# Layer 2 attention of a four-layer kernel: scores in two passes, with the maximum carried into the second one by DMA

## The chip, the cores and the metric

The kernel runs on one core of a Trainium2 chip. A core has five engines with a queue each: TensorE (PE in the profile; its weight loads are PEld), VectorE (DVE), ScalarE (ACT), GpSimd (POOL) and SyncE (SP), which here issues the DMAs. The metric is the device time of one execution in microseconds (us); the median of three runs of the kernel before is 3875.83 us.

## The reference, cut to what matters

Four layers run over 4 sequences of 1024 tokens of width 256. The change lies in the attention of the second one (`_L0_ffn_ref`), which has 8 heads of 64 and a causal mask:

```python
sim = jnp.einsum('bhid,bhjd->bhij', q * SCALE, k)
sim = jnp.where(causal_mask, jnp.finfo(sim.dtype).min, sim)
attn = jax.nn.softmax(sim, axis=-1)
out = jnp.einsum('bhij,bhjk->bhik', attn, values)
```

A softmax subtracts the largest score of each query before the exponential. The kernel computes the scores with the keys on partitions, so a query's maximum has to be subtracted along the free axis; it does that inside the matmul sum.

## The kernel before, in words

For each sequence, layer 2 runs three blocks: `gates_and_values`, `attention` and `output_experts`. No engine starts a block before all have finished the one ahead. The change is in `attention`; it adds 8 matmuls at the end of `gates_and_values`.

`attention` first projects two heads at a time: a group c is four products (K and Q, each for 512 tokens), `project` on PE. Each lands in a PSUM bank; ACT rounds it to a shorter format, fp32r (`hi_parts`), and DVE subtracts to get what the rounding lost (`lo_parts`). From the second group on all four products use one bank, so `project` waits for `qk_parts`, the end of DVE's part for the product before it. `kst` holds a head's keys as rounded part in 64 partitions and lost part in the other 64; `qst` holds the rounded queries in both halves; `qlo` the lost part of the queries in both halves.

A head then goes through three kinds of work on PE, each in 8 pieces k = 0 to 7, one per 128 keys or queries:

- `maxima` (L648, L650): rounded scores of 128 queries against the keys up to them, 1024 columns at k = 0 down to 128 at k = 7. DVE reduces each to one number per query (L769, `mx`).
- `scores` (L662 to L666): 12 units of up to 512 columns for the 8 pieces, 1024 columns at k = 0 down to 128 at k = 7. Each unit is a product with `qst` (L662), a product with `qlo` (L663), on the diagonal the mask (L665), and a product of `negones` with `shift` (L666), which subtracts the maximum. `shift` is a diagonal matrix of the maxima that POOL writes from `mx` (L785), eight instructions per head. ACT takes the exponential (L703, `prob`).
- `weighted` (L674): `prob` times the values in full fp32, into bank `PV`. At a head's end ACT copies the row of denominators (`den_out`, L725) and DVE the output (`head_out`, L759); the next head's first `weighted` waits for both.

The order is written out by hand on every engine. Step by step, the scores of one head run in the same step as the maxima of the next, piece by piece, and in every second step the four projections of a later group lie between them. A head's scores follow its last maxima directly, in the next step. Where the text says "step of head h" it means from the first score product of h to that of h+1: projections fall in those of heads 0, 2 and 4, and no maxima are left in that of head 7.

PE waits in its own queue for `shift_ready` before a head's first score, for `exp_ready` (three banks) before later ones, and for `max_read` before a piece of maxima, since those share two pairs of half-banks.

Layer 3 has a step of the same sort as the one that the change brings here. Its SP queue moves maxima out of a column of `peak` into one row of `qst` (L1274), 128 elements of 4 bytes per DMA and 8 DMAs in a row; its products L1303 then wait for them.

Of the kernel before, what the change touches and what calls it, by code (L numbers as in the profile page):

```python
# [421 lines left out]
ATTN2 = ("qk_mm qk_hi qk_parts max_mm max_read shift_ready score_mm exp_ready pv_mm o_read den_read "  # L422
# [6 lines left out]
def layer2(nc, ctx, m, I, src, dst):  # L429
# [39 lines left out]

    def gates_and_values(own):  # L470
# [14 lines left out]
        with nc.Block() as block:  # L485
# [7 lines left out]
            def _(pe):  # L493
# [7 lines left out]
                for n, (h, t) in enumerate(order):  # L501
# [10 lines left out]
                    last.then_inc(s.value_mm, 1)  # L512

# [76 lines left out]
    def attention(own, b):  # L590
# [6 lines left out]
        mx = sb("mx", [P, H0, NT])  # L597
# [5 lines left out]
        parts = [(kind, n) for kind in "kq" for n in range(NH)]  # L603
        part_at = {0: 0, 1: 1, 2: 2, 4: 3}
# [10 lines left out]
        with nc.Block() as block:  # L615
            @block.sync
            def _(sp):
                fetch_load(sp, m, s, src[(b + 1) % SEQS])
                sp.dma_start(oe[:, :, :], I["oe2"][:, 0]).then_inc(s.oe_in, 16)
                for h in range(H0):  # L620
                    sp.wait_ge(s.den_read, h + 1)
                    sp.dma_start(dens[h:h + 1, :], den[den_row(h), h % 2, :]).then_inc((s.even_den_out, s.odd_den_out)[h % 2], 16)
                sp.wait_ge(s.even_den_out, 16 * (H0 // 2))
                sp.wait_ge(s.odd_den_out, 16 * (H0 // 2))
                sp.wait_ge(s.oe_in, 16)

            @block.tensor
            def _(pe):
# [10 lines left out]
                def maxima(h, k):  # L639
                    t = NT - 1 - k  # L640
                    if k == 0:
                        pe.wait_ge(s.qk_parts, 4 * (h // 2 + 1))
# [10 lines left out]
                def scores(h, k):  # L653
                    for n, (kk, lo, hi) in enumerate(units, U * h):
                        if kk != k:
                            continue
                        if n % U == 0:
                            pe.wait_ge(s.shift_ready, NT * (h + 1))
                        if n >= 3:
                            pe.wait_ge(s.exp_ready, n - 2)  # L660
                        out, keys = bank(m.ps, n % 3, 0, hi - lo), kst[:, h % RK, k * P:(k + 1) * P]
                        pe.matmul(out, keys, qst[:, h % RK, lo:hi], start=True, stop=False)  # L662
# [15 lines left out]
                for step in range(H0 + 2):  # L678
                    h1, h2 = step - 1, step - 2
                    for k in range(NT):  # L680
                        if h2 >= 0:
                            scores(h2, k)
                        if step % 2 == 0 and step < H0 and k in part_at:
                            project(step // 2, part_at[k])
                        if 0 <= h1 < H0 and k < NT - 1:
                            maxima(h1, k)
                        if h2 >= 0 and k >= 1:
                            weighted(h2, k - 1)
                        if 0 <= h1 < H0 and k == NT - 2:
                            maxima(h1, NT - 1)  # L690
                    if h2 >= 0:
                        weighted(h2, NT - 1)

            @block.scalar
            def _(act):
# [10 lines left out]
                def hi_parts(c, j):  # L706
# [5 lines left out]
                    for odd in (0, 1):  # L712
                        got, slot = bank(m.ps, proj_bank(c, j), 0, HALF, half(odd)), (2 * c + odd) % RK
                        if kind == "k":
                            last = act.copy(kst[half(odd), slot, cols], got)
# [11 lines left out]
                for step in range(H0 + 2):  # L727
                    h2 = step - 2
                    for k in range(NT):
                        if h2 >= 0:  # L730
                            exps(h2, k)
                        if k == 0 and h2 >= 1:
                            den_out(h2 - 1)
                        if k == 3 and step == H0 + 1:
                            fetch_sd(act, m, s)
                        if step % 2 == 0 and step < H0 and k in part_at:
                            hi_parts(step // 2, part_at[k])
# [3 lines left out]
            def _(dve):  # L741
                def lo_parts(c, j):
# [3 lines left out]
                    for odd in (0, 1):  # L746
# [4 lines left out]
                        else:  # L751
                            for to in (0, 1):
                                last = dve.tensor_tensor(qlo[half(to), slot, cols], got, qst[half(odd), slot, cols].bitcast(F32),
                                                         ALU.subtract)
# [6 lines left out]
                for step in range(H0 + 2):  # L761
                    h1, h2 = step - 1, step - 2
                    for k in range(NT):
                        if k == 0 and h2 >= 1:
                            head_out(h2 - 1)
                        if 0 <= h1 < H0:
                            t = NT - 1 - k
                            dve.wait_ge(s.max_mm, NT * h1 + k + 1)
                            dve.reduce_max(mx[:, h1, t:t + 1], bank(m.ps, max_bank(h1, k), 0, (t + 1) * P), AX_X).then_inc(s.max_read, 1)  # L769
                        if step % 2 == 0 and step < H0 and k in part_at:  # L770
                            lo_parts(step // 2, part_at[k])
# [5 lines left out]
            def _(pool):  # L777
                clear(pool, s1)
                for h in range(H0):
                    if h >= 2:  # L780
                        pool.wait_ge(s.score_mm, U * (h - 1))
                    for k in range(NT):
# [1111 lines left out]
```

## Time and profile before

| | |
|---|---|
| median of 3 runs | 3875.83 us (3875.41 to 3878.35) |
| profiled execution: time | 3882.36 us |
| profiled execution: span | 3880.6 us |
| PE busy | 3373.7 us, 87% |
| DVE / ACT / POOL busy | 2080.9 / 1466.3 / 830.2 us |
| layer 2's attention, four times | 206.1, 206.8, 205.2 and 206.5 us |
| of these, PE busy | 188.5, 189.2, 187.6 and 188.9 us |

The profile gives the share of the span in which each engine worked, groups of instructions by line, and, for any stretch, the instructions in order of time with the idle time before each and what ended it. The granted clock (PEclk) is the share of TensorE's full speed that the chip gave in a stretch: 1.00 is 2.4 GHz and 0.50 is 1.2 GHz. Matmul ends are modelled: a 512-column product is shown with 0.39 us, while the next one starts 0.23 us after it, so the cost of a product on PE is the distance between two starts. Below that is called its slot.

### The profile page before, as it was taken

Reading aid. Unit: us, or ns where it says so; the run is one execution under the profiler, and the core shown is the slowest. Engines: PE = TensorE matmul, PEld = TensorE weight load, DVE = VectorE, ACT = ScalarE, POOL = GpSimd, SP = SyncE. Lnnn points to the kernel's source line nnn. Section 1 sums busy time; section 2 is a strip of 40 time slices with the busy share of each in tenths; the row PEclk is TensorE's granted clock in tenths of the full one; section 3 lists DMA queues with packets and bytes.
Section 4 is the critical chain, followed back from the end, with each engine's and each line's share of the span. In section 5 each row is a group of like instructions: output and inputs, shape, how many; then the busy total and the mean of one; then the engine's idle time right before and its main releaser. Section 6 shows DMA issues by size and latency. Waiting matters only on the chain. (4 is left out here: it accounts for less than half of the span.)

```text
span 3880.6 us, 51281 instructions
## 1 busy us (share of the span) xinstructions
PE 3373.7 (87%) x18610; PEld 2435.7 (63%) x18610; DVE 2080.9 (54%) x3463; ACT 1466.3 (38%) x2638; POOL 830.2 (21%) x908
## 2 busy tenths in 40 slices
PE   6996898988988989888989698998988789888898
PEld 4555655975568755875569445555454477777776
DVE  4446744686455954667446574655647434343333
ACT  2321144412443134421444355463644433333333
POOL 1112322742246411643127101001010000000000
PEclk9997899988998999998999789898998899899999
DMA  5111100110011100210001200000001120000000
GB/s 179 41 45 60 38 1 30 45 45 22 1 51 47 44 1 1 74 34 33 1 30 48 63 2 13 12 7 18 2 12 12 61 94 6 17 11 12 11 12 11
DMA packets 139735, 121.01 MB, mean 31 GB/s; under 512 B 79696, under 2 KB 121936, under 8 KB 136016
## 3 DMA queue, kind: packets, MB, share of 16 engines
q1 hardware_dynamic: 139472, 117.45, 9.9%
q8 instruction: 172, 2.82, 0.3%
q14 instruction: 91, 0.75, 0.1%
HBM read 100.23 MB, written 28.31 MB: 33 GB/s over the span
## 5 line engine op out<-in xcount | busy, mean ns | idle before, releaser
L1375 ACT ACTIVATE l3b_prob<-sums 128x512 f32<-128x512 f32 (+3 forms) x768 | 337.8, 497 | 280.7 <-PE sums L1308 224.3
L1623 PE MATMUL sums<-l4a_uhi,l_h 128*128 128x512 f32 x1024 | 405.2, 396 | 0.0
L1623 PE MATMUL sums<-l4a_ulo,l_h 128*128 128x512 f32 x1024 | 404.0, 395 | 0.0
L842 POOL TENSOR_TENSOR l2c_rlo<-l2c_routed,l2c_rhi 128x512 fp32r<-128x512 f32 x256 | 348.1, 1373 | 216.0 <-ACT l2c_rhi L868 178.6
L769 DVE TENSOR_REDUCE l2b_mx<-sums 128x1 f32<-128x1024 f32 (+7 forms) x256 | 192.1, 758 | 316.5 <-PE sums L650 315.8
L703 ACT ACTIVATE l2b_prob<-sums 128x512 f32<-128x512 f32 (+3 forms) x384 | 186.4, 491 | 394.8 <-PE sums L666 390.0
L1668 DVE TENSOR_TENSOR l4a_ulo<-l4a_made,l4a_uhi 128x512 fp32r<-128x512 f32 x192 | 132.3, 689 | 375.2 <-ACT l4a_uhi L1636 374.3
L222 POOL COPY sb_x<-sb_nx 128x2048 f32<-128x2048 f32 x12 | 23.0, 1914 | 1383.6 <-issue 604.6
L952 PE MATMUL sums<-l2c_ohi,l2c_rhi 128*128 128x256 f32 x1024 | 295.2, 288 | 12.8 <-POOL l2c_rlo L842 11.9
L1303 PE MATMUL sums<-l_qst,l_kst 64*128 64x512 f32 (+3 forms) x768 | 290.6, 440 | 17.2 <-DMA l_qst<-l3b_peak 9.9
L674 PE MATMUL sums<-l2b_prob,l_vx 128*128 128x512 f32 (+3 forms) x768 | 301.0, 506 | 3.3 <-ACT l2b_den L725 1.9
L952 PE MATMUL sums<-l2c_ohi,l2c_rlo 128*128 128x256 f32 x1024 | 292.7, 286 | 0.0
L952 PE MATMUL sums<-l2c_olo,l2c_rhi 128*128 128x256 f32 x1024 | 292.6, 286 | 0.0
L1286 PE MATMUL sums<-l_kst,l_qst 64*128 64x512 f32 (+3 forms) x768 | 244.5, 459 | 46.7 <-DVE l3b_peak L1387 21.6
L785 POOL TENSOR_SCALAR l2b_shift<-sb_ident,l2b_mx 128x128 fp32r<-128x128 f32 x256 | 154.2, 605 | 603.7 <-DVE l2b_mx L769 494.3
L905 DVE TENSOR_TENSOR l2c_routed<-l_oT,sums 128x512 f32<-128x512 f32 x256 | 171.7, 683 | 151.3 <-PE sums L942 148.0
L1303 PEld LDWEIGHTS sums<-l_qst,l_kst 64*128 64x128 f32 x768 | 147.2, 207 | 162.0 <-ACT l3b_prob L1375 130.7
L868 ACT CAST l2c_rhi<-l2c_routed 128x512 fp32r<-128x512 f32 x256 | 158.1, 621 | 239.9 <-DVE l2c_routed L905 238.9
L203 PE MATMUL sums<-sb_ident,sb_nx 128*128 128x128 f32 x256 | 61.1, 422 | 193.2 <-issue 92.7
L1623 PEld LDWEIGHTS sums<-l4a_uhi,l_h 128*128 128x128 f32 x1024 | 192.3, 188 | 47.3
L1623 PEld LDWEIGHTS sums<-l4a_ulo,l_h 128*128 128x128 f32 x1024 | 192.3, 188 | 46.1
L510 PE MATMUL sums<-l2a_vhi,l2a_xhi 128*128 128x512 f32 x512 | 204.8, 400 | 10.7 <-POOL l2a_vlo L574 6.3
(247 smaller groups left out, 8170.7 us busy)
## 6 DMA issues: line engine op xcount, KB each, us to landing
l_ve<-ve SPq DMA_DIRECT2D x34, 512.0 KB, 4.1
l_oe<-oe SPq DMA_DIRECT2D x16, 1024.0 KB, 5.9
sb_nx<-sums SPq DMA_DIRECT2D x15, 1024.0 KB, 5.6
l2c_word<-weights_copy SPq DMA_DIRECT2D x32, 352.0 KB, 3.6
weights_copy<-h SPq DMA_DIRECT2D x2, 4096.0 KB, 26.2
l_qst<-l3b_peak SPq DMA_DIRECT2D x512, 0.5 KB, 2.0
l_h<-weights_copy SPq DMA_DIRECT2D x2, 4096.0 KB, 23.9
sb_nx<-tokens SPq DMA_DIRECT2D x5, 1024.0 KB, 5.6
```

The costliest lines, as they stand in the source:

```text
L510: last = pe.matmul(bank(m.ps, n % RING), x[:, c, t * P:(t + 1) * P], v[:, h % 2, c, :], start=(c == 0 and x is xhi and v is vhi), stop=(c ...
L674: last = pe.matmul(bank(m.ps, PV, lo, hi), vx[:, k, h, :], prob[:, k % 2, lo:hi], start=(k == 0), stop=True, skip_group_check=True)
L703: act.activation(prob[:, k % 2, lo:hi], bank(m.ps, n % 3, 0, hi - lo), ACT.Exp, scale=SCALE0).then_inc(s.exp_ready, 1)
L769: dve.reduce_max(mx[:, h1, t:t + 1], bank(m.ps, max_bank(h1, k), 0, (t + 1) * P), AX_X).then_inc(s.max_read, 1)
L842: pool.tensor_tensor(rlo[:, i % RT, :], routed[:, i % RT, :], rhi[:, i % RT, :].bitcast(F32), ALU.subtract).then_inc(s.routed_lo, 1)
L868: act.copy(rhi[:, i % RT, :], routed[:, i % RT, :]).then_inc(s.routed_hi, 1)
L905: dve.tensor_tensor(routed[:, i % RT, :], oT[:, c, n * HALF:(n + 1) * HALF], bank(m.ps, 4 + i % 4), ALU.mult).then_inc(s.routed, 1)
L952: last = pe.matmul(m.ps[:, t * D:(t + 1) * D], r[:, k % RT, cols], w[:, c % 2, e, :], start=(c == e == 0 and t % 2 == 0 and r is rhi and w ...
L1286: last = pe.matmul(bank(m.ps, at, 0, hi - lo), qst[rows(a), p, t * P:(t + 1) * P], kst[rows(a), p, lo:hi], start=True, stop=True)
L1303: last = pe.matmul(bank(m.ps, part % SCORE, 0, hi - lo), kst[rows(a), p, k * P:(k + 1) * P], qst[rows(a), p, lo:hi], start=True, stop=True)
L1375: act.activation(prob[:, i % RB, j, a, 0:hi - lo], bank(m.ps, part % SCORE, 0, hi - lo), ACT.Exp, scale=SCALE1).then_inc(s.exp_ready, 1)
L1623: run(lambda out, a, x, first, last: pe.matmul(out, a, x, start=first, stop=last))
```

## The change

The product with `qlo` and the product of `negones` with `shift` become one. `krow` holds the rounded keys of a head in partitions 0 to 63 and the constant -1 in partition 64; `qrow` holds the lost part of the queries in 0 to 63 and the maxima, as a row, in 64. One product over these 65 partitions (L701) adds the lost part and subtracts the maximum. (Lost part times lost part, which the `qlo` product had as well, is no longer in the sum.)

- PE: 12 products fewer per head. Maxima of a head end two pieces ("ticks", `WAIT = 2`) before its scores start.
- SP: 8 new DMAs per head (L651) take a column of `mx`, 128 elements of 4 bytes in 128 partitions, to a stretch of the row. The first waits until all eight maxima of the head are read; the head's first score waits for all eight to land. The DMA of the denominators stands behind them.
- POOL: its 8 instructions per head and the tile `shift` go; one memset per sequence writes the row of -1.
- ACT: four copies instead of two per K product (`kst` and `krow`). DVE: two subtractions instead of four per Q product. The products go in the order K0, K1, Q1, Q0, in ticks 2 to 5 instead of 0, 1, 2 and 4.
- DVE's `head_out` and ACT's `den_out` stand behind the reduction and the copies of their tick; before, they stood ahead of them (`den_out` ahead of the copies).
- The first head's maxima wait for all rounded parts and two lost parts, no longer for all four lost parts.
- PE gets 8 products that nobody reads (`warm`) at the end of `gates_and_values`, 8 behind the first four projections, and one behind each piece of the first head's maxima.

```diff
-        kst, qst, qlo = (sb(n, [P, RK, T], F32R) for n in ("kst", "qst", "qlo"))
-        shift = sb("shift", [P, 2, T], F32R)
+        kst, qst = sb("kst", [P, RK, T], F32R), sb("qst", [P, RK, T], F32R)
+        krow, qrow = sb("krow", [P, RK, T], F32R), sb("qrow", [P, RK, T], F32R)
+        ROWS = DH0 + 1
...
-        parts = [(kind, n) for kind in "kq" for n in range(NH)]
-        part_at = {0: 0, 1: 1, 2: 2, 4: 3}
+        parts = [("k", 0), ("k", 1), ("q", 1), ("q", 0)]
+        WAIT = 2
+        part_at = {WAIT + j: j for j in range(4)}
+        ticks = NT * (H0 + 2) + WAIT + 1
+        scored_in = lambda x: divmod(x - 2 * NT - WAIT, NT)
+        peaked_in = lambda x: divmod(x - NT, NT)
...
+                for h in range(H0):
+                    sp.wait_ge(s.max_read, NT * (h + 1))
+                    if h >= 2:
+                        sp.wait_ge(carried[h % 2], carried_to(h - 2))
+                    if h >= RK:
+                        sp.wait_ge(s.score_mm, U * (h - RK + 1))
+                    for t in range(NT):
+                        sp.dma_start(qrow[DH0:ROWS, h % RK, t * P:(t + 1) * P].bitcast(F32),
+                                     mx[:, h, t:t + 1].bitcast(F32)).then_inc(carried[h % 2], 16)
+                    if h >= 1:
+                        den_row_out(h - 1)
...
                         if n % U == 0:
-                            pe.wait_ge(s.shift_ready, NT * (h + 1))
+                            pe.wait_ge(s.qk_parts, 4 * (h // 2 + 1))
+                            pe.wait_ge(carried[h % 2], carried_to(h))
+                            pe.wait_ge(s.row_ready, 1)
...
-                        pe.matmul(out, keys, qlo[:, h % RK, lo:hi], start=False, stop=False)
...
-                        pe.matmul(out, m.negones[:, :], shift[:, h % 2, lo:hi], start=False, stop=True).then_inc(s.score_mm, 1)
+                        pe.matmul(out, krow[0:ROWS, h % RK, at], qrow[0:ROWS, h % RK, lo:hi], start=False,
+                                  stop=True).then_inc(s.score_mm, 1)
...
+                for x in range(ticks):
+                    h2, k2 = scored_in(x)
+                    h1, k1 = peaked_in(x)
+                    if has(h2):
+                        scores(h2, k2)
+                    if project_in(x):
+                        project(*project_in(x))
+                        if x == 3:
+                            warm(pe, 6, 8)
+                    if has(h1):
+                        maxima(h1, k1)
+                        if h1 == 0:
+                            warm(pe, PROJ, 1)
+                    h2, k2 = scored_in(x - 1)
+                    if has(h2):
+                        weighted(h2, k2)
...
+                            act.copy(kst[half(odd), slot, cols], got)
+                            last = act.copy(krow[half(0), slot, cols], got)
...
+                            last = dve.tensor_tensor(qrow[half(0), slot, cols], got, qst[half(odd), slot, cols].bitcast(F32),
+                                                     ALU.subtract)
...
+                    if has(h1):
+                        t = NT - 1 - k1
+                        dve.wait_ge(s.max_mm, NT * h1 + k1 + 1)
+                        dve.reduce_max(mx[:, h1, t:t + 1], bank(m.ps, max_bank(h1, k1), 0, (t + 1) * P), AX_X).then_inc(s.max_read, 1)
+                    if project_in(x):
+                        lo_parts(*project_in(x))
+                    if k2 == 0 and 1 <= h2 < H0:
+                        head_out(h2 - 1)
```

What PE's queue holds where one head's scores end and the next head's begin. Before: the last maxima of the next head (L648 with 128 columns), the last score unit of this one, two weighted products (L674), and the next head's first scores.

```order
L648 MATMUL sums<-l2b_kst,l2b_qst 128x128
L650 MATMUL sums<-sb_mask_qk,sb_ident 128x128
L662 MATMUL sums<-l2b_qst,l2b_kst 128x128
L663 MATMUL sums<-l2b_qlo,l2b_kst 128x128
L665 MATMUL sums<-sb_mask_kq,sb_ident 128x128
L666 MATMUL sums<-l2b_shift,sb_negones 128x128
L674 MATMUL sums<-l2b_prob,l_vx 128x256
L674 MATMUL sums<-l2b_prob,l_vx 128x128
L662 MATMUL sums<-l2b_qst,l2b_kst 128x512
```

After, at the same place; the next head's last maxima (L682 with 128 columns) stand seven rows higher still, with a weighted product of 512 columns and the score unit of 256 columns behind them.

```order
L684 MATMUL sums<-sb_mask_qk,sb_ident 128x128
L710 MATMUL sums<-l2b_prob,l_vx 128x384
L698 MATMUL sums<-l2b_qst,l2b_kst 128x128
L700 MATMUL sums<-sb_mask_kq,sb_ident 128x128
L701 MATMUL sums<-l2b_qrow,l2b_krow 128x128
L682 MATMUL sums<-l2b_kst,l2b_qst 128x512
L682 MATMUL sums<-l2b_kst,l2b_qst 128x384
L684 MATMUL sums<-sb_mask_qk,sb_ident 128x128
L710 MATMUL sums<-l2b_prob,l_vx 128x256
L698 MATMUL sums<-l2b_qst,l2b_kst 128x512
```

Between a head's last maxima and its first scores there now lie two ticks: three weighted products, two score units and the first two pieces of the maxima of the head after it.

SP's queue in the attention block. Before, after the two large loads there are only the rows of the denominators:

```order
L121 ISA
L121 DMA sb_nx<-sums 128x8x256
L619 DMA l_oe<-oe 128x2048
L622 DMA l_dens<-l2b_den 1x16x64 [waits l2_attn_den_read] x8
L615 UNCONDITIONAL_BRANCH [waits l2_attn_oe_in,l2_attn_odd_den_out,l2_attn_even_den_out]
```

After, heads 0 and 1, and the start of head 2:

```order
L639 DMA l_oe<-oe 128x2048
L651 DMA l2b_qrow<-l2b_mx 1x128x1 [waits l2_attn_max_read]
L651 DMA l2b_qrow<-l2b_mx 1x128x1 x7
L651 DMA l2b_qrow<-l2b_mx 1x128x1 [waits l2_attn_max_read]
L651 DMA l2b_qrow<-l2b_mx 1x128x1 x7
L642 DMA l_dens<-l2b_den 1x16x64 [waits l2_attn_den_read]
L651 DMA l2b_qrow<-l2b_mx 1x128x1 [waits l2_attn_even_carried,l2_attn_max_read]
```

Eight issues with one wait ahead of them came in per head, and each row of denominators now stands behind the next head's eight.

## Rows read from the trace of the kernel before

**Rows 1.** Stretches: start:end and length, busy us (count) by engine, PEclk, DMA

```profile
448.80:472.90 24.10, 15.73 (x36) 7.79 (x36) 14.11 (x20) 6.96 (x12) 4.79 (x8) 0.71 0.26 87
...
571.40:600.40 29.00, 26.23 (x107) 15.06 (x105) 15.63 (x22) 13.74 (x25) 4.79 (x8) 1.00 0.00 1
600.40:619.10 18.70, 18.70 (x88) 11.92 (x88) 7.11 (x9) 6.79 (x13) 4.85 (x8) 1.00 0.00 1
...
637.90:654.90 17.00, 16.16 (x70) 10.11 (x68) 8.18 (x30) 9.54 (x16) 0.00 (x0) 1.00 0.01 1
```

**Rows 2.** Timeline of PE: start us, us, instruction, idle before; first scores of head 5

```profile
600.38 0.50 PE L662 MATMUL sums<-l2b_qst,l2b_kst 128*128 128x512 f32 x1 [0.19 <-POOL l2b_shift L785]
600.72 0.39 PE L663 MATMUL sums<-l2b_qlo,l2b_kst 128*128 128x512 f32 x1
600.96 0.23 PE L665 MATMUL sums<-sb_mask_kq,sb_ident 128*128 128x128 bf16 x1
```

**Rows 3.** Timeline of PE: the end of the same step

```profile
611.93 0.80 PE L662 MATMUL sums<-l2b_qst,l2b_kst 128*128 128x512 f32 x1
...
615.49 1.08 PE L674 MATMUL sums<-l2b_prob,l_vx 128*128 128x512 f32 x2
616.00 0.68 PE L662 MATMUL sums<-l2b_qst,l2b_kst 128*128 128x256 f32 x1
616.52 0.28 PE L663 MATMUL sums<-l2b_qlo,l2b_kst 128*128 128x256 f32 x1
616.64 0.23 PE L665 MATMUL sums<-sb_mask_kq,sb_ident 128*128 128x128 bf16 x1
...
619.14 0.50 PE L662 MATMUL sums<-l2b_qst,l2b_kst 128*128 128x512 f32 x1
```

**Rows 4.** Layer 3's carry on SP: timeline, and the landing times of line L1274

```profile
2229.97 4.98 SPq L1274 DMA_DIRECT2D l_qst<-l3b_peak  x8
...
2236.40 0.47 SPq L1274 DMA_DIRECT2D l_qst<-l3b_peak  x1
...
DMA to landing us min/median/max: 1.9/2.0/3.9
```

**Rows 5.** Instructions of head 5's step by shape: busy us, mean ns, idle before

```profile
L759 DVE COPY l_oT<-sums 64x1024 f32<-64x1024 f32 x1 | 1.2, 1217 | 1.0 <-PE sums L674 1.0
...
L769 DVE TENSOR_REDUCE l2b_mx<-sums 128x1 f32<-128x768 f32 x1 | 1.0, 958 | 2.3 <-PE sums L650 2.3
```

**Rows 6.** Timeline of all engines: projections and last maxima, head 4's step

```profile
578.18 1.98 PE L635 MATMUL sums<-l_xT,l_wk 128*128 128x512 f32 x4 [1.34 <-DVE l2b_kst L749]
...
590.78 1.88 PE L635 MATMUL sums<-l_xT,l_wq 128*128 128x512 f32 x4
...
592.69 2.36 ACT L718 CAST l2b_qst<-sums 64x512 fp32r<-64x512 f32 x4 [1.12 <-PE sums L635]
...
595.08 2.79 DVE L753 TENSOR_TENSOR l2b_qlo<-sums,l2b_qst 64x512 fp32r<-64x512 f32 x4 [1.39 <-ACT l2b_qst L718]
...
598.69 0.23 PE L650 MATMUL sums<-sb_mask_qk,sb_ident 128*128 128x128 bf16 x1
...
598.96 0.29 DVE L769 TENSOR_REDUCE l2b_mx<-sums 128x1 f32<-128x128 f32 x1 [0.16 <-PE sums L650]
```

**Rows 7.** Stretches, columns as in rows 1: around two idle stretches of PE

```profile
2361.00:2363.30 2.30, 0.67 (x10) 0.58 (x11) 0.00 (x0) 0.89 (x3) 0.00 (x0) 1.00 0.07 1
2363.50:2366.70 3.20, 3.20 (x28) 2.10 (x24) 0.00 (x0) 2.29 (x6) 0.00 (x0) 0.50 0.00 0
3410.00:3412.50 2.50, 0.00 (x0) 0.00 (x0) 2.50 (x8) 0.00 (x0) 0.00 (x0) 1.00 0.06 21
3412.70:3416.00 3.30, 3.30 (x15) 2.67 (x16) 3.30 (x6) 3.20 (x6) 0.00 (x0) 1.00 0.00 0
```

**Rows 8.** Timeline: the first head's maxima and their reductions, sequence 1

```profile
463.84 1.22 PE L648 MATMUL sums<-l2b_kst,l2b_qst 128*128 128x512 f32 x2 [6.38 <-DVE l2b_qlo L753]
...
465.23 2.22 DVE L769 TENSOR_REDUCE l2b_mx<-sums 128x1 f32<-128x1024 f32 x2 [1.45 <-PE sums L650]
```

More of the change, by code:

```diff
@@ L468, in layer2, with warm @@
     fetch_first(nc, m, s0, src[0], load, prepare)
+    def warm(pe, at, times):
+        for _ in range(times):
+            pe.matmul(bank(m.ps, at), sel[:, 0, :], sel[:, 0:HALF // P, :], start=True, stop=True)
     def gates_and_values(own):
@@ L602, in attention, with project_in @@
         through = lambda k: sum(kk <= k for kk, _lo, _hi in units)
-        parts = [(kind, n) for kind in "kq" for n in range(NH)]
-        part_at = {0: 0, 1: 1, 2: 2, 4: 3}
+        parts = [("k", 0), ("k", 1), ("q", 1), ("q", 0)]
[4 more added lines that the diff above has]
+        peaked_in = lambda x: divmod(x - NT, NT)
+        has = lambda h: 0 <= h < H0
+        carried = (s.even_carried, s.odd_carried)
+        carried_to = lambda h: 16 * NT * (h // 2 + 1)
+        def project_in(x):
+            step, k = divmod(x, NT)
+            if x < 4:
+                return 0, x
+            if step and step % 2 == 0 and step < H0 and k in part_at:
+                return step // 2, part_at[k]
         MAX, PV, PROJ = 3, 5, 7
@@ L725, in den_out @@
                     act.copy(den[den_row(h), h % 2, :], bank(m.ps, PV, 0, T, den_row(h))).then_inc(s.den_read, 1)
[L727 to L737, printed above, removed]
+                for x in range(ticks):
+                    h2, k2 = scored_in(x)
+                    if has(h2):
+                        exps(h2, k2)
+                    if project_in(x):
+                        hi_parts(*project_in(x))
+                    if k2 == 0 and 1 <= h2 < H0:
+                        den_out(h2 - 1)
+                    if (h2, k2) == (H0 - 1, 3):
+                        fetch_sd(act, m, s)
                 den_out(H0 - 1)
@@ L759, in head_out @@
                     dve.tensor_copy(oT[vcol(h), h // 2, :], bank(m.ps, PV, 0, T, vcol(h))).then_inc(s.o_read, 1)
[L761 to L771, printed above, removed]
+                for x in range(ticks):
+                    h2, k2 = scored_in(x)
+                    h1, k1 = peaked_in(x)
+                    if has(h1):
+                        t = NT - 1 - k1
+                        dve.wait_ge(s.max_mm, NT * h1 + k1 + 1)
+                        dve.reduce_max(mx[:, h1, t:t + 1], bank(m.ps, max_bank(h1, k1), 0, (t + 1) * P), AX_X).then_inc(s.max_read, 1)
+                    if project_in(x):
+                        lo_parts(*project_in(x))
+                    if k2 == 0 and 1 <= h2 < H0:
+                        head_out(h2 - 1)
                 fetch_stats(dve, m, s)
@@ L778, in _ @@
                 clear(pool, s1)
[L779 to L782, printed above, removed]
-                        t = NT - 1 - k
-                        pool.wait_ge(s.max_read, NT * h + k + 1)
-                        pool.tensor_scalar(shift[:, h % 2, t * P:(t + 1) * P], m.ident[:, :], mx[:, h, t:t + 1], None,
-                                           ALU.mult).then_inc(s.shift_ready, 1)
+                pool.memset(krow[DH0:ROWS, :, :].bitcast(F32), -1.0).then_inc(s.row_ready, 1)
     def output_experts(own, b):
```

34 lines of the change are left out of this document (9 added, 25 removed).

## The prediction

> **What bounds the kernel now.** I read the stretches of layer 2's attention first [rows 1]. The step of head 5, without projections, lasts 18.7 us and PE is busy in all of it; ACT works 6.8 us of it, DVE 7.1. So PE sets the pace there, and a product less is time won as long as nothing makes PE wait. The step of head 4, with four projections, lasts 29.0 us and leaves PE idle for 2.8; the timeline names the rounding of the projections for half of that [rows 6]. The head of the block takes 24.1 us at a mean granted clock of 0.71. The last step, 17.0 us, has scores and weighted products alone. Per sequence that is the head, one step of 32 us (head 0), two of 29, four of 18.75, and 17: 206 us. Then I read what the new wait will cost, from the place in layer 3 where the same transfer is made [rows 4], and how the clock answers idle stretches [rows 7].
>
> **The product that goes.** A lost-part product of 512 columns has a slot of 0.24 us (600.72 to 600.96) [rows 2], one of 256 has 0.12 [rows 3]; those of 384 and 128 are taken as 0.18 and 0.11. A head has 6, 2, 2 and 2 of them: 1.44 + 0.24 + 0.36 + 0.22 = 2.25 us. That lies on PE, the bound, and 32 heads make 72 us. The product with the row of maxima takes the place of the one with `shift`: as many columns, so no change. POOL's eight instructions go, and with them the wait of about 0.2 us at a head's first score [rows 2]. A step without projections thus holds 18.75 - 2.25 - 0.2 = 16.3 us of PE work. The memset of the -1 row, 4096 elements in one partition, would take 5 us at the rate of DVE's copy of 1024 [rows 5] and runs on an idle POOL during the 24 us of the head.
>
> **The carry that comes.** From the last maxima product of a head to its reduced maximum pass 0.56 us (598.69 to 598.96, and 0.29 more) [rows 6]. SP then issues eight DMAs. Layer 3 does exactly this: eight issues take 4.98 us, one every 0.64, each lands 2.0 us after its issue, and the next group, which waits for the last landing, starts 6.43 us after the first [rows 4]. Shape and size are the same (128 elements of 4 bytes from 128 partitions into one row), so I take 6.43. With 0.1 at each end for the hand-over, as between PE and DVE in rows 6, the next head's first score starts 7.1 us after the last maxima product ends. Cover: before, 3.65 us lie between 615.49 and 619.14 [rows 3]. The two ticks that now stand there hold the same weighted products and score units without two lost-part products (0.23), without the smaller maxima of 256 and 128 columns (0.35) and the last weighted product (0.3), but with the maxima of 1024 and 896 columns, four products of 0.23 or less and two masks, 1.0 together: 3.8 us. Exposed at each head: 7.1 - 3.8 = 3.3 us. That is more than the 2.25 won. Behind PE's wait stand the next maxima, so DVE and ACT stand too, and nothing catches up later.
>
> **The weighted product's wait.** `head_out` now stands behind the reduction of 768 columns in its tick. From the first score: scores 1.05 and maxima 0.43, 0.2 to hand over, 0.96 and 1.22 on DVE [rows 5], so the head's first weighted product can start 3.9 us in; PE would be there at 3.2. It costs 0.7 in steps without projections; where projections hold PE up anyway, nothing.
>
> **Steps without projections** (heads 1, 3, 5, 6): 16.3 + 3.3 + 0.7 = 20.3 against 18.75: +1.55, four of them +6.2.
>
> **Steps with projections.** All four share a bank, so the next starts only when the rounding of the last is through. In rows 6 the fourth starts at 590.78, DVE's part at 595.08, 4.30 later, behind four ACT copies. The change makes that four copies for every product and two DVE subtractions (half of the 2.79): 4.30 + 1.40 + 0.05 = 5.75 us from start to start. PE's own work between two projections is 3.7 to 5.2 us, so the chain bounds. Before, a K product needed two copies only. The step: 1.05 of scores, three times 5.75, the fourth projection 1.75, then what PE still has to do up to the last maxima, about the 4.1 us of 611.93 to 616.00 [rows 3], which holds the same kinds of work; then 7.1 for the carry: 31.2 against 29.0, +2.2. For heads 2 and 4 that is +4.4.
>
> **The last step** has no carry behind it: 17.0 - 2.1 = 14.9 (0.1 of the 2.25 kept for its waits on exponentials).
>
> **The head.** The maxima wait for ACT's last copy and no longer for DVE's last subtraction, and DVE's queue is two subtractions shorter per Q product. The reductions begin at about 463.2 instead of 465.23 [rows 8], and the clock may be up for the first projections thanks to the unread products, 1.6 us more in perhaps half the cases. The reductions then end near 469.5 and the carry brings the first score to 475.6, against 472.9 [rows 1]: +2.7. The unread products themselves stand in waits of 4 to 6 us. Head 0's step is 31.2 and some 2 us for a low clock after the idle carry, against 30.6 to 32.0: +1.9.
>
> Sum per sequence: 2.7 + 1.9 + 6.2 + 4.4 - 2.1 = 13.1; four make +52 us.
>
> **The clock.** PE now idles some 3 us before every head's first score. In the trace such stretches have gone both ways [rows 7]: after an idle stretch of 1.9 us ending at 2362.6 the clock was 0.50 for the next 3.2 us, with PE busy throughout; after 2.85 us ending at 3412.6 it stayed at 1.00. Of 17 idle stretches of 1.9 to 2.9 us, 10 were followed by a fall; of nine of 3.0 to 3.4 all were. A fall costs half of some 3.4 us, 1.7, less the 0.7 of the weighted product's wait, which it hides. I take 1 us for each of seven heads: +7 per sequence, +28. Bounds: nothing, and 2.5 us per head where two stretches in a row are slow, +70.
>
> In all +80 us. The profiled execution would go from 3882.4 to 3962; the median of the runs, 6.5 us lower, from 3875.8 to **3956**.
>
> **A rule against the measured rows.** By the trace a group of eight is in place after 6.4 us [rows 4]. The Trainium skill, "DMA: Bandwidth & Descriptors", section "Rules for kernel authors", says to issue a DMA early and wait late, since its fixed setup cost overlaps with compute. Read as one fixed cost for the group, the carry would fit under two ticks and the sum would be that of the first rival; the rows show the issues in series instead.
>
> **Rivals.** (1) The carry is hidden: the issues are short here and the group lands 2.1 us after its start. The gap is then 2.8 us, less than the cover of 3.8; steps without projections fall to 17.0 (-7.0 for four), those of heads 2 and 4 to 28.2 (-1.6), the last to 14.9 (-2.1), the head gains 1.6 and head 0's step 1.1: -13.4, four times -54: **3822**. It decides from an issue of (3.8 - 2.8) / 7 = 0.14 us down. For it speaks only that SP has little else to do; against it, 512 issues of 0.6 us. Chance 0.08. (2) The carry is exposed but the clock holds, as at 3412: 3876 + 52 = **3928**. Chance 0.22. (3) Every stall brings two slow stretches, and the waits of 1 to 2 us in the projections bring more: +52 + 90 = **4018**. Chance 0.12. (4) Carry half hidden, gains and losses level: within 8 us of 3876. Chance 0.04. The forecast itself: 0.54.
>
> **Numbers.** Median 3956. The forecast and rival 2 lie between 3910 and 3985 with their unknowns (0.7 or nothing for the weighted product, 6.4 or the 7 us of a disturbed group, 0.5 to 1.5 us of clock per head); a part of rival 3 is taken in: 3908 to 4005. Faster by over 0.2% (8 us, what a measurement can tell): 0.08; within: 0.04; slower: 0.88.
>
> **What would show it.** Right: SP with eight issues of 0.6 us behind each head's last maximum; PE idle for about 3 us before L698 of each head, ended by the DMA to `l2b_qrow`; steps of 20 to 22 and 31 to 34 us; a PEclk under 1.00 in the attention's middle; PE busy some 60 us less in all, clock apart. Wrong: issues of 0.1 us, or a first score that waits for nothing; then it is rival 1. If the steps with projections are much shorter than 31 us, my chain through the rounding is mis-sized.

## The result, and the profile after

The changed kernel takes 3966.5 us (median of four runs, 3961.4 to 3970.5) where the kernel before takes 3875.6 (3869.5 to 3878.4): a ratio of 1.0236, with 1.0218 to 1.0254 as the interval. It is slower, and the forecast of 3956 was 10 us short. The profiled execution has a span of 3968.7 us against 3880.6.

First the page's totals of after: busy time, share of the span, instructions.

```profile
span 3968.7 us, 50755 instructions
...
PE 3363.5 (85%) x18322; PEld 2402.9 (61%) x18322; DVE 2034.3 (51%) x3399; ACT 1498.2 (38%) x2702; POOL 688.9 (17%) x656
```

PE runs 288 instructions fewer than before (18322 against 18610) and is busy 10 us less (3373.7 before), yet the span is 88 us longer. So PE works less and waits more. Attention, from the first projection to the last weighted product, went from 206.1, 206.8, 205.2 and 206.5 us in the four sequences to 227.8, 228.7, 232.1 and 229.1: +93 us in all. The rest of the kernel is 5 us shorter; in it layer 3, whose code did not change, is 10 us shorter and the other parts together 5 longer.

The stretches of sequence 1 in the columns of [rows 1], which they answer: the head of the block, then the steps of heads 0, 3, 4, 5 and the last one; behind them 3.2 us shortly after head 3's first score, the end of head 4's step, and the 3.3 us behind that.

```profile
451.50:477.70 26.20, 18.39 (x58) 9.39 (x58) 13.51 (x18) 9.08 (x16) 3.50 (x1) 0.91 0.26 80
477.80:513.10 35.30, 28.07 (x90) 14.26 (x91) 11.47 (x16) 14.84 (x28) 0.00 (x0) 0.88 0.02 1
567.20:588.20 21.00, 18.18 (x76) 11.04 (x77) 7.18 (x9) 6.78 (x13) 0.00 (x0) 0.92 0.03 1
588.20:621.20 33.00, 26.02 (x92) 13.45 (x93) 12.69 (x17) 15.72 (x29) 0.00 (x0) 0.95 0.02 1
621.30:641.50 20.20, 16.88 (x76) 9.84 (x76) 7.09 (x9) 6.67 (x13) 0.00 (x0) 1.00 0.03 0
662.00:679.30 17.30, 16.53 (x58) 9.89 (x58) 8.17 (x30) 9.64 (x16) 0.00 (x0) 0.84 0.01 1
568.60:571.80 3.20, 3.20 (x13) 2.44 (x12) 2.08 (x2) 2.41 (x5) 0.00 (x0) 0.50 0.00 0
618.80:621.10 2.30, 0.00 (x0) 0.00 (x0) 0.57 (x1) 0.00 (x0) 0.00 (x0) 1.00 0.10 1
621.30:624.60 3.30, 3.30 (x18) 2.29 (x18) 1.62 (x2) 2.40 (x4) 0.00 (x0) 1.00 0.00 0
```

In [rows 1] the step of head 5 had PE busy for all of its 18.7 us. Now it is busy for 16.9 of 20.2: less work, more time. The last three rows are the clock's: PE does nothing for 2.3 us before head 5's first score and goes on at full clock; before head 3's it idles as long (2.49 us, next view), and the clock is 0.50 in the 3.2 us shown, with PE busy throughout.

The timeline around head 3's first score (all engines, shortened) shows what PE waits for. It answers [rows 3] for the cover and [rows 4] for the carry.

```profile
560.07 0.23 PE L684 MATMUL sums<-sb_mask_qk,sb_ident 128*128 128x128 bf16 x1
560.14 1.08 PE L710 MATMUL sums<-l2b_prob,l_vx 128*128 128x512 f32 x2
560.65 0.68 PE L698 MATMUL sums<-l2b_qst,l2b_kst 128*128 128x256 f32 x1
560.67 4.98 SPq L651 DMA_DIRECT2D l2b_qrow<-l2b_mx  x8
561.41 0.64 PE L682 MATMUL sums<-l2b_kst,l2b_qst 128*128 128x512 f32 x2
562.16 1.22 DVE L803 TENSOR_REDUCE l2b_mx<-sums 128x1 fp32r<-128x1024 f32 x1 [1.52 <-PE sums L684]
563.44 0.68 PE L682 MATMUL sums<-l2b_kst,l2b_qst 128*128 128x512 f32 x2 [0.37 <-DVE l2b_mx L803]
564.02 0.65 PE L710 MATMUL sums<-l2b_prob,l_vx 128*128 128x256 f32 x2
567.16 0.47 PE L698 MATMUL sums<-l2b_qst,l2b_kst 128*128 128x512 f32 x1 [2.49 <-issue]
```

The last maxima product of head 3 starts at 560.07. SP begins its eight issues at 560.67 and spends 4.98 us on them. The last transfer lands at 567.07, 6.40 after the first issue, and PE's first score follows at 567.16. PE's own work for the two ticks between ran out at 564.67. The page labels the 2.49 us "<-issue", that is, it names no releaser; the landing is known from the records of the DMA, and where PE stands at the same wait in experiment 4, the page names the DMA to `l2b_qrow`. From L684 to L698 pass 7.09 us here, and 7.05 to 7.15 at 30 of the 32 heads.

Before head 7's first score PE idles longer, 4.17 to 4.19 us in all four sequences, though the carry takes no longer:

```profile
657.17 0.65 PE L710 MATMUL sums<-l2b_prob,l_vx 128*128 128x256 f32 x2
662.00 0.77 PE L698 MATMUL sums<-l2b_qst,l2b_kst 128*128 128x512 f32 x1 [4.18 <-issue]
```

No head follows, so no maxima lie in the two ticks and the cover is shorter. For the same reason head 6's step holds less work than those of heads 1, 3 and 5.

All issues together, by count and with the least, the median and the longest duration in ns, and the time from issue to landing:

```profile
L651 SPq DMA_DIRECT2D l2b_qrow<-l2b_mx x256: 469/601/1373, 471.2 to 2081.7; - x128
...
DMA to landing us min/median/max: 1.9/2.0/2.8
```

The other two waits that the prediction names. The first is in head 6's step; the kernel lets this weighted product start only behind `head_out` (L795), `den_out` and the exponentials of its piece:

```profile
644.29 1.23 DVE L795 COPY l_oT<-sums 64x1024 f32<-64x1024 f32 x1
...
645.62 0.67 PE L710 MATMUL sums<-l2b_prob,l_vx 128*128 128x512 f32 x1 [0.68 <-ACT l2b_prob L740]
```

The page names ACT, but the copy L795 ends at 645.52 and PE starts 0.10 later; `den_out` ended at 644.57 and the exponentials of the piece at 643.49. So it is `head_out` that PE waits for. The second is in head 4's step:

```profile
592.93 0.58 ACT L752 CAST l2b_kst<-sums 64x512 fp32r<-64x512 f32 x1 [2.46 <-PE sums L668]
...
594.60 0.58 ACT L753 CAST l2b_krow<-sums 64x512 fp32r<-64x512 f32 x1
...
595.21 1.39 DVE L786 TENSOR_TENSOR l2b_kst<-sums,l2b_kst 64x512 fp32r<-64x512 f32 x2 [0.90 <-ACT l2b_krow L753]
...
596.66 0.70 PE L668 MATMUL sums<-l_xT,l_wk 128*128 128x512 f32 x1 [2.12 <-DVE l2b_kst L786]
```

DVE can begin only at 595.21, behind the copies into `kst` and into `krow`, and the next projection waits 2.12 us for it at 596.66. In [rows 6] the like wait was 1.34.

### The profile page after: what moved, and what is told of

It is laid out like the page before. It is cut to its first block and busy times, and to the rows that moved or that the text cites. A ratio compares the mean times of both kernels' runs of the same rounds, so it can differ in the third digit from the quotient of the medians.

```text
span 3968.7 us, 50755 instructions
## 1 busy us (share of the span) xinstructions
PE 3363.5 (85%) x18322; PEld 2402.9 (61%) x18322; DVE 2034.3 (51%) x3399; ACT 1498.2 (38%) x2702; POOL 688.9 (17%) x656
## 5 line engine op out<-in xcount | busy, mean ns | idle before, releaser
L803 DVE TENSOR_REDUCE l2b_mx<-sums 128x1 fp32r<-128x1024 f32 (+7 forms) x256 | 191.8, 756 | 425.8 <-PE sums L684 424.9
L710 PE MATMUL sums<-l2b_prob,l_vx 128*128 128x512 f32 (+3 forms) x768 | 311.0, 516 | 4.8 <-ACT l2b_prob L740 4.8
L698 PE MATMUL sums<-l2b_qst,l2b_kst 128*128 128x512 f32 (+3 forms) x384 | 225.8, 588 | 91.8 <-issue 91.8
```

The lines of the kernel that those rows point to most:

```text
L698: pe.matmul(out, kst[:, h % RK, at], qst[:, h % RK, lo:hi], start=True, stop=False)
L710: last = pe.matmul(bank(m.ps, PV, lo, hi), vx[:, k, h, :], prob[:, k % 2, lo:hi], start=(k == 0), stop=True, skip_group_check=True)
```

## The experiments

**1. Is it the carry's place, or its being there at all?** Each DMA is issued as soon as its own maximum is read, from the largest piece down. The DMA of a head's denominators, which stood behind the eight, moves with them: it now stands in the middle of a later head's.

```
             for h in range(H0):
-                sp.wait_ge(s.max_read, NT * (h + 1))
...
-                for t in range(NT):
+                for k in range(NT):
+                    t = NT - 1 - k
+                    sp.wait_ge(s.max_read, NT * h + k + 1)
                     sp.dma_start(qrow[DH0:ROWS, h % RK, t * P:(t + 1) * P].bitcast(F32),
...
-                    if h >= 1:
-                        den_row_out(h - 1)
+                        if k == 3 and h >= 2:
+                            den_row_out(h - 2)
+                den_row_out(H0 - 2)
...
```

> The changed kernel with one edit: each of a head's eight DMAs is issued as soon as its own maximum is read, instead of all eight behind the last one. Theory A (the eight issues in series behind the last maximum are what costs, 7.1 us from the last maxima product to the first score against 3.8 us of cover): only the last issue and its landing remain behind the last maximum, 0.56 + 0.6 issued and landed in 2.0, so about 2.8 us, less than the cover. PE no longer idles before a head's first score; 3.3 us and the low clock go at seven heads, somewhat more at the first, four sequences: 3825 to 3860 us. Theory B (the stall is only where other costs of the new order show, such as the longer rounding chain or the later output copies): PE waits elsewhere instead and the time stays above 3900 us.

Measured: 3839.8 us against 3872.5, a ratio of 0.992 (0.990 to 0.994). The moment at which the same 256 DMAs are issued turns 91 us of loss into 33 of gain. The timeline at the same place of a step (sequence 2, before head 2):

```profile
959.74 0.66 PE L684 MATMUL sums<-l2b_kst,l2b_qst 128*128 128x512 f32 x2 [0.37 <-DVE l2b_mx L805]
959.76 0.47 SPq L652 DMA_DIRECT2D l2b_qrow<-l2b_mx  x1
...
960.31 0.65 PE L712 MATMUL sums<-l2b_prob,l_vx 128*128 128x256 f32 x2
...
960.61 0.58 PE L700 MATMUL sums<-l2b_qst,l2b_kst 128*128 128x512 f32 x1
```

No idle time stands before the first score of any head. The steps of heads 1, 3 and 5 take 17.6 us, that of head 6 16.1, those of heads 2 and 4 28.6 to 30.3. From the last maxima product to the first score now pass 4.25 us (2.6 for head 7) instead of 7.09. The rows of the denominators were moved too, and that part wasn't tried apart; but in after PE starts 0.1 us behind the landing of the eighth DMA, and no score waits for a row of denominators. Attention is 194 to 198 us per sequence instead of 228 to 232.

**2. Is it an amount of cover?** The issue stays late, and the distance from a head's last maximum to its scores grows from two ticks to three.

```
-        WAIT = 2
-        part_at = {WAIT + j: j for j in range(4)}
+        WAIT = 3
+        part_at = {2 + j: j for j in range(4)}
```

> The changed kernel with three ticks instead of two between a head's last maxima and its first scores; the projections stay in ticks 2 to 5 and the eight DMAs stay behind the last maximum. Theory A: the chain stays 7.1 us, the cover grows from 3.8 to 5.7 us, so about 1.4 us stay exposed in steps without projections and none where a projection falls into the third tick; with fewer falls of the clock some 70 us less than the changed kernel, 3880 to 3915 us. Theory B: no change beyond 10 us, since the wait moves to another place.

Measured: 3885.9, a ratio of 1.0031 (1.0012 to 1.005). A tick more takes back 81 us. Steps without projections are 18.2 to 18.9 us; idle stretches of 0.9 to 2.2 are left before some first scores and one of 2.6 before head 7's. Both runs say that the exposed carry, with what hangs on it, is the loss.

**3. Does the price go by issues or by bytes?** Every DMA is cut in two of 64 elements: the same bytes, 16 issues a head.

```
                 for t in range(NT):
-                    sp.dma_start(qrow[DH0:ROWS, h % RK, t * P:(t + 1) * P].bitcast(F32),
...
+                    for part in (0, 1):
+                        at = t * P + HPART * part
+                        sp.dma_start(qrow[DH0:ROWS, h % RK, at:at + HPART].bitcast(F32),
...
```

> The changed kernel with each DMA of the carry split into two of 64 elements, sixteen per head. If an issue costs 0.64 us whatever it moves, the chain grows by 8 x 0.64 = 5.1 us per head, 32 heads 164 us: 4120 to 4150 us. If an issue costs by the element, the sixteen take as long as the eight: 3960 to 3975 us.

Measured, one run: 4151.3 us, 185 above after, for 256 issues more. A half costs as much to issue as a whole:

```profile
L653 SPq DMA_DIRECT2D l2b_qrow<-l2b_mx x512: 463/597/1630, 472.2 to 2263.2; - x171
```

597 ns against 601. From the last maxima product to the first score pass 11.9 us instead of 7.1: eight issues more take 4.8, 0.60 each, or 154 us for 32 heads. So the price is one of issues. The other 31 fit the clock, which is at 0.50 for 85 to 102 us of attention per sequence instead of 34 to 51.

**4. What does the clock take?** Ten unread products stand ahead of each head's wait for the carry, so that PE is busy where it would idle. The time of the carry isn't touched.

```
                             pe.wait_ge(s.qk_parts, 4 * (h // 2 + 1))
+                            warm(pe, PROJ, 10)
                             pe.wait_ge(carried[h % 2], carried_to(h))
```

> The changed kernel with ten more unread products on PE ahead of each head's wait for the carried row (2.3 us at full clock, inside the wait of 2.5 us and more). The wait itself stays. Clock theory: nothing falls any more before heads 1 to 6, steps without projections go from 21.05 to 20.32 us, and the falls in the steps with projections and at the first head are fewer: 25 to 40 us less than the changed kernel, 3926 to 3942 us. Rival: the clock costs nothing, since other waits absorb it: 3960 to 3970 us.

Measured: 3940.3, a ratio of 1.0174 (1.0155 to 1.0192): 26 us under after. The steps of heads 0, 1 and 2 in sequence 2, columns as in [rows 1]:

```profile
941.05:972.36 31.31, 26.44 (x100) 14.39 (x100) 11.47 (x16) 14.71 (x28) 0.00 (x0) 1.00 0.02 0
972.36:992.72 20.36, 19.28 (x87) 11.83 (x87) 7.09 (x9) 6.67 (x13) 0.00 (x0) 1.00 0.03 1
992.72:1024.06 31.34, 26.67 (x103) 14.62 (x103) 12.70 (x17) 15.61 (x29) 0.00 (x0) 1.00 0.02 1
```

With the clock at 1.00 a step without projections is 20.36 us and one with them 31.3, whereas after has 21 to 22 and 33 or more where the clock fell. Of the 91 us the falls that went are thus worth 26 by the medians; attention alone is 36 us shorter in the profiled executions (881 against 918 in all). Neither is the whole price of the clock: 7 of 30 falls behind the first head's first score are left, and the unread products push that first score back by 0.9 to 1.1 us (8.02 to 8.23 from the last maxima product instead of 7.12 to 7.15). The rest, 57 to 65 us, is waits, less the product's gain.

**5. What is the removed product worth?** The kernel before, without its product with `qlo`. It leaves the lost part of the queries out of the scores, and nothing comes in its place.

```
                        pe.matmul(out, keys, qst[:, h % RK, lo:hi], start=True, stop=False)
-                       pe.matmul(out, keys, qlo[:, h % RK, lo:hi], start=False, stop=False)
```

> The kernel before without the product of keys with the lost part of the queries, which is left out of the sum; all else is as before. It prices the product alone. Theory A (PE is the bound and each head's twelve products are worth 2.25 us): 32 x 2.25 = 72 us less, 3800 to 3812 us. Theory B (maxima, exponentials or the projections' rounding take over as the bound): less than half of that, above 3840 us.

Measured: 3841.7, a ratio of 0.9917 (0.9895 to 0.9938): 31 us, not 72. A step without projections falls by 1.63 us (18.75 to 17.12), not by 2.25; one with projections by 0.64 (28.98 to 28.34), since there other waits grow, those for the roundings and for the reductions: PE's idle time in such a step goes from 2.8 to 3.8 us. In head 3's step the clock fell in each sequence (18.4 to 18.5 us at a mean of 0.91), which takes most of the gain back there. PE's waits over about 120 us of sequence 2 (us in total, times, longest), in this kernel:

```profile
PE sums L648 <- DVE l2b_mx L768: 4.0, 5, 1.5
```

and in the kernel before:

```profile
PE sums L648 <- DVE l2b_mx L769: 2.5, 2, 1.3
```

With less to do between, PE comes to the next maxima before DVE has read the last. One such place, timeline of PE and DVE in sequence 1:

```profile
599.31 1.22 DVE L768 TENSOR_REDUCE l2b_mx<-sums 128x1 f32<-128x1024 f32 x1 [0.95 <-PE sums L650]
...
600.59 0.67 PE L648 MATMUL sums<-l2b_kst,l2b_qst 128*128 128x512 f32 x2 [0.31 <-DVE l2b_mx L768]
```

The next maxima start when the 1.22 us reduction ends, and PE has stood 0.31. In the kernel before, the lost-part products filled that: such a step had no idle time at all. From start to start this one place takes 0.40 us more than before, which is two thirds of the 0.6 by which 1.63 falls short of the slots.

**6. The unread products, under a late carry.** After, without them.

```
-                warm(pe, 7, 8)
...
-                        if x == 3:
-                            warm(pe, 6, 8)
...
-                        if h1 == 0:
-                            warm(pe, PROJ, 1)
```

> The changed kernel without the unread products. Prediction's view: they stand in waits and only lift the clock for the first projections, 1.6 us in half the cases, so without them 0 to 4 us more per sequence: 3966 to 3982 us. Rival: they delay the first head's maxima, since one stands behind each piece, and the time falls to 3950 to 3962 us.

Measured: 3984.0, a ratio of 1.0278 (1.0254 to 1.0302), 17 us over after. The profiled executions agree on the direction only: layer 2 is 4 us longer, and layer 3, whose code is the same in both, 16 (948.6 against 932.9). All four runs are slower than all four of after, but only 4 us are found in the layer that was edited. So neither the size nor, for certain, the sign is shown here; experiment 9 is the better test.

**7. The copy into `krow` moved to GpSimd.** It copies from `kst`, as soon as ACT has rounded, and leaves ACT two copies per K product. Once with the late issue:

```
-                            act.copy(kst[half(odd), slot, cols], got)
-                            last = act.copy(krow[half(0), slot, cols], got)
+                            last = act.copy(kst[half(odd), slot, cols], got)
...
+                        pool.wait_ge(s.qk_hi, 4 * c + j + 1)
+                        for odd in (0, 1):
...
+                            last = pool.tensor_copy(krow[half(0), slot, cols], kst[half(odd), slot, cols].bitcast(F32))
...
```

> The changed kernel (late issue) with the krow copies on GpSimd only. Chain theory: the same 5 to 7 us per sequence as in e5, since the steps with projections are a chain and the carry comes behind it: 3938 to 3948 us. Rival: a wait that the carry then takes over, no gain: above 3958 us.

Measured: 3954.3, a ratio of 1.0202 (1.0185 to 1.022), 12 us under after and between the two expectations. Steps with projections fall to 31.1 to 32.5 us, but from the first score on 35 to 43 us per sequence go at half clock against 29 to 41, which can take part of it back.

**8. Both together:** experiment 1 and this copy.

> Early issue of the DMAs as in e1_early, and GpSimd instead of ScalarE copies the rounded keys into krow, so that a K product has two ScalarE copies in its chain again (a start-to-start distance of 4.6 us instead of 5.75). Chain theory: the two K distances in each of three steps with projections shrink by 1.15 us where PE has no other work, 5 to 7 us per sequence, 3812 to 3822 us against 3840 of e1_early. Rival: GpSimd's copies come late or slow VectorE down, and nothing is gained: 3835 us or more.

Measured: 3799.6, a ratio of 0.9819 (0.9796 to 0.9842). It beats both kernels, by 76 and by 167 us, and is under what either reason expected, since no fall of the clock is left behind the first score (2 or 3 per sequence in experiment 1, 6 to 8 in after). The steps of heads 1 and 2 in sequence 2, columns as in [rows 1]:

```profile
926.57:944.19 17.62, 16.71 (x78) 9.95 (x77) 7.09 (x10) 6.67 (x13) 0.00 (x0) 1.00 0.04 1
944.19:970.88 26.69, 23.85 (x95) 12.74 (x93) 12.71 (x18) 13.48 (x25) 2.44 (x4) 1.00 0.03 1
```

The step with projections is 26.7 us, 2.3 under that of before [rows 1], for 2.44 us of copies on GpSimd, which has nothing else to do there. Attention is 185 to 186 us per sequence.

**9. The unread products, under a hidden carry.** Experiment 8 without them.

> e5_early_poolk without the unread products. If they lift the clock at the block's head only, their loss is 0 to 4 us per sequence in that head and nothing elsewhere: 3800 to 3816 us. Rival: the 17 us by which e3_no_unread was slower than the changed kernel are theirs, 3815 us or more. Third: they cost as much as they give, 3795 to 3800 us.

Measured: 3821.1, a ratio of 0.9857 (0.9839 to 0.9875), 21 us over experiment 8. Here the traces agree with the times: layer 2 is 17.5 us longer (1759.9 against 1742.4), the head 22.0 to 25.2 us against 20.2 to 21.9, head 0's step 28.2 to 28.9 against 26.6, and every later step the same.

**10. The weighted product's wait.** On top of experiment 8, `head_out` goes ahead of the reduction in its tick, and the first and last weighted products ahead of the maxima.

```
+                    if k2 == 0 and 1 <= h2 < H0:
+                        head_out(h2 - 1)
                     if has(h1):
                         t = NT - 1 - k1
                         dve.wait_ge(s.max_mm
...
-                    if k2 == 0 and 1 <= h2 < H0:
-                        head_out(h2 - 1)
...
+                    first = has(h3) and k3 in (NT - 1, 0)
+                    if first:
+                        weighted(h3, k3)
                     if has(h1):
                         maxima(h1, k1)
...
+                    if has(h3) and not first:
+                        weighted(h3, k3)
```

> e5_early_poolk with the order changed in two of a head's ticks: PE runs the last weighted product of the old head and the first of the new one ahead of the maxima of their ticks, and VectorE copies the old head's output ahead of that tick's reduction. If the wait of 0.7 us at a head's first weighted product is real, it goes in the four steps without projections, 2 to 3 us per sequence: 3786 to 3792 us against 3800 of e5. Rival: the maxima behind it wait instead, for the reduction that now comes later, and nothing is gained: 3797 to 3805 us.

Measured: 3831.8, a ratio of 0.9885 (0.9865 to 0.9906), 32 us worse than experiment 8; both expectations missed. The wait at the head's first weighted product shrinks from 0.54 us to 0.17 to 0.20 in the steps of heads 1, 3 and 5 and goes in head 6's, and with it 0.1 and 0.4 us of the step. But the steps of heads 2 and 4 grow from 26.7 us to between 29.5 and 31.2, and head 0's from 26.6 to between 28.3 and 32.8. PE's waits from 900 to 1080 us (in total, times, longest), here:

```profile
PE sums L670 <- DVE l2b_kst L790: 10.5, 6, 2.3
PE sums L684 <- DVE l2b_mx L809: 4.5, 9, 1.3
```

and in experiment 8:

```profile
PE sums L670 <- DVE l2b_kst L787: 4.0, 3, 1.5
...
PE sums L684 <- DVE l2b_mx L804: 2.2, 6, 0.4
```

On DVE the 1.2 us copy now stands in front of the reductions and of the roundings that the next projection waits for. Which of the two moves did it wasn't tried apart.

## Why the prediction was right, and where its terms were off

**What bounds and what comes.** The mechanism was as forecast: the carry is serial in its issues, longer than its cover, and PE stands before every first score. 7.1 us from the last maxima product to the first score were forecast, 7.05 to 7.15 measured; 6.43 for a group, 6.37 to 6.47 measured from its first issue to its last landing (both at 30 of 32 heads). That the total came within 10 us is in part luck, since errors in its terms cancel. Layer 3's own rows were the right place to read that price [rows 4]. Rival 1 needed issues of 0.14 us; they take 0.60.

**The removed product was mis-sized, 2.25 us a head.** Experiment 5 shows 1.63 in steps without projections. The slots themselves are right (2.23 from start to start); they were added up as if PE would never run into another wait.

**The 0.2 at a head's first score doesn't belong there.** The wait in [rows 2] ends at 600.38 and so lies in the step of head 4, with projections. The step behind it is busy for 18.70 of 18.70 us in [rows 1]; there was nothing to take off, and 16.3 was too little for that reason too.

**The exposed carry was mis-sized, 3.3 us.** PE idles 2.44 to 2.51 us before most first scores. From start to start the carry costs more, 7.09 - 4.25 = 2.8 us, with experiment 1 for the step without it, since a product is shown longer than its slot. The cover of 3.8 was a sum of slots alone: they are about 3.9 of the 4.25, and the other 0.37 is a wait for the reduction (959.74 in experiment 1). These errors cancel. Experiment 1 has 16.7 us of PE busy in such a step (forecast 16.3) and 0.9 of waits (forecast 0.7); with 2.8 for the carry that makes 20.4. Measured were 20.3 to 20.4 where the clock held, forecast 20.3.

**Head 6's step** was counted as one of four alike. It has two pieces of maxima less and that much more of exposed carry, 16.1 + 4.2 = 20.3, so the sum is the same; that, too, wasn't foreseen.

**The weighted product's wait.** 0.7 forecast, with `head_out` as the cause and the product 3.9 us into the step. Measured are 0.54 in the steps of heads 1, 3 and 5 at full clock and 0.68 in head 6's, with the product 3.9 to 4.2 us in, each time 0.10 behind the end of `head_out` (as at 644.29 and 645.62), in experiments 1 and 4 as well. Where the clock has just fallen, the wait is gone, as forecast. Experiment 10 has `head_out` earlier and the wait all but gone.

**Steps with projections.** 31.2 forecast, 31.3 at full clock (experiment 4), 33.0 to 33.8 and once 35.5 in after with the clock's falls. The chain of roundings was forecast with 5.75 us from one projection to the next; at full clock the three distances are 5.64, 5.75 and 5.85. Its other end confirms it: without ACT's copies into `krow` the first two are 4.8, and the step falls from 28.6 us or more (experiment 1) to 26.7 (experiment 8).

**The last step.** 14.9 forecast. Its shortest is 15.65 (experiment 4), and 15.67 in experiment 5, 1.3 under before: again the product, counted at 2.1.

**The head and head 0's step.** +2.7 and +1.9 forecast, +1.4 and +4.1 measured. The sum, 5.5, is near 4.6; the split isn't. The wait for head 0's carry has nothing but unread products beside it, PE idles 3.6 us before the first score, and the clock is down for part of head 0's step each time (a mean of 0.84 to 0.87). The forecast's own sum for the head is 0.5 short as well: reductions that end at 469.5 and a carry of 6.43 with 0.2 of hand-over give 476.1, not 475.6.

**The clock.** 28 us forecast, 26 to 36 by experiment 4. All 22 idle stretches of 2.44 to 2.51 us before the first scores of heads 1 to 6 began at full clock; in or up to 2 us behind 19 of them it fell to 0.50, where [rows 7] and their like had 10 of 17.

**PE's busy time.** I expected some 60 us less in all, clock apart. It is 10 less. "Clock apart" can't be read off that number, and the unread products are in it; it was a poor sign to name.

**The rivals.** Rival 2 (clock holds, 3928) is nearest to experiment 4, 3940, where the clock still fell 7 times. Rival 1 (carry hidden, 3822) is experiment 1, 3840, so its sum was 18 short. Most of that is in the steps of heads 2 and 4: 28.2 forecast, 28.6 at full clock and 29.2 to 30.3 with a fall of the clock, which came in seven of eight, together 12 us; the steps without projections (17.0 forecast, 17.6 and once 16.1 measured) make 4. Its 28.2 doesn't follow from its terms either, which give 31.2 - 3.3 = 27.9. Rival 3 didn't come.

**The sum.** Per sequence, the clock's share in each: steps without projections +9, those of heads 2 and 4 +9, head and head 0 together +5.5, the last step 0. Measured between first projection and last weighted product is +23.3, forecast 13.1 + 7 = 20. Four times 3.3 make 13 us too little; the other stages, 5 us shorter, bring it to the 8 by which the profiled execution (3970.5 us) is above the forecast for it (3962).

**The rule.** The Trainium skill, "DMA: Bandwidth & Descriptors", section "Rules for kernel authors", says to issue early and wait late. Experiment 1 does exactly that and is 127 us faster than the kernel that issues all eight behind the last maximum. Here the rule wins not by overlapping one fixed cost but by spreading the issues over a step in which SP is idle. Spread out, an issue takes 0.47 us in the median of that run's trace:

```profile
L652 SPq DMA_DIRECT2D l2b_qrow<-l2b_mx x256: 468/469/605, 465.8 to 1947.5; - x128
```

## What to carry to other kernels

A group of small DMAs costs its issues in series on the queue's engine. Here that was 0.61 to 0.63 us for each issue but the last, plus one landing of 2.0 us: 6.4 for eight, 11.2 for sixteen. Issue each when its own data is there instead of all behind the last. When work is taken from the engine that sets the pace, count the waits that it was covering; here 2.25 us of products were worth 1.63, and 0.64 where other waits stood behind them. Unread products in idle time that can't be avoided were worth 21 us (experiment 9) and 26 (experiment 4) here, by keeping the clock up.

## What the runs showed of the hardware that was not expected

- A DMA issue on SP takes 601 ns in the median for 128 elements of 4 bytes and 597 for 64 where issues follow each other, and 469 ns in experiment 1, where most stand alone.
- With idle stretches of 2.44 to 2.51 us the granted clock fell from 1.00 to 0.50 in 19 of 22 cases. Why the other three held isn't known.
- Layer 3, with the same code, took 931 to 953 us between the profiles of these kernels. A difference of 10 us between two profiles doesn't belong to an edit unless it is found in the stretch that was edited.
